# Expert loop: tokens copied and split ahead; last query block in halves; a home of their own for the row indices

## The chip, the cores and the metric

The kernel runs on one core of one Trainium2 chip, as one launch. The metric is the device time of one execution in microseconds (us). The core has TensorE (matmuls), VectorE, ScalarE, GpSimd and SyncE. Each has its own instruction stream; semaphores tie them together.

## The reference, cut to what matters

The layer works on x of 8 x 512 tokens with 256 channels, all in float32. It normalises the tokens and adds to x a windowed attention (16 heads of 16 channels, windows of 128 at a stride of 64, of which the output keeps the first four windows of each batch) and a mixture of experts (8 experts, the best two for each token):

```python
xn = _layernorm(x)
# attention: per window softmax(q k^T / 4) v, then @ w_out + b_out; o[:, :512]
scores = xn @ gate_w.T;  top 2 of 8, softmax over the two -> total_probs
h12 = xn @ w12[e].T;  h1, h2 = halves of 512
hidden = silu(h1) * h2
expert_out = hidden @ w3[e].T
x = x + attention(xn) + sum_e total_probs[e] * expert_out
```

The kernel computes only the chosen experts: tokens are sorted by expert into 71 tiles of 128 rows.

## The kernel before, in words

There are three stages. First come the layer norm, the transposes, the gates and attention of batches 0 and 1, during which the slots of the tokens and the list of row indices (the map) are made. Then the expert loop runs over 71 tiles. Then follow attention batches 2 to 7, in which the rows that the experts wrote to HBM (`ys_scratch`) are read back, scaled and added. Each batch has 8 units `u` (half a window's heads each), so that two units are one window of 128 queries.

The order is written out by hand, for each engine on its own.

Expert loop. A tile `j` is worked with buffers of parity `k`. GpSimd gathers 128 rows by `GIDX` into `XS` and scatters results by `SIDX`. TensorE, for each `k`: `up(j+1, 0)` (6 matmuls of 512 columns), `turn_hidden(j)` (4 transposes, line 1450), `up(j+1, 1)` (6 matmuls), `tokens(j+2)` (2 transposes, line 1428), `down(j)` (8 records). ScalarE: `high_part(j+2, half 0)` (line 829, the weights rounded to fp32r), `take_tanh(j+1)` (841), `take_ht(j)` (845), `high_part(j+2, half 1)`, `take_xt(j+2)` (849, copies the turned tokens to `XTS`), `take_y(j)` (855, into `SIDE` or `OTS`). VectorE: `low_part(j+2, half 0)` (350, weights minus their high part), the two products of `hidden(j+1)` (1172, then `tt` at 897), `low_xt(j+2)` (897, the tokens' low part, which releases `up(j+2, 0)`), `low_part(j+2, half 1)`. `high_part` and `low_part` first load the tile's expert number from `EJ` into a register (`weights_of`, lines 341 to 344). `up(j, half)` waits for `low_ready[half]`, and `up(j, 0)` also for `xt_free`.

Indices. `GIDX` and `SIDX` lie in `WORK`, where attention's `REST` is written by `split`. So `finish_map`, which writes them, stands a unit after `take_map` and waits for the parts of batch 2; and in batch 2 VectorE waits for `y_stored`, GpSimd's signal that all scatters have finished, before its first `split`.

End of a window. ScalarE copies the sums to `SIDE` and the counts to `DENS` (760, 761; in the trace `DENS` is part of `XN`). VectorE inverts `DENS` (1062), GpSimd multiplies into `OTS` (574), TensorE projects with `WOUT`, VectorE adds the total (`project`, 897 on `XN`). SyncE stores a batch of 512 rows with one transfer (`send`, 459). In the last batch VectorE projects window 2 before it inverts for window 3.

Of the kernel before, what the change touches and what calls it, by code (L numbers as in the profile page):

```python
# [97 lines left out]
def layer(nc, x, wqkv, bqk, bv, wout, bout, gate, wexp, out):  # L98
    with ExitStack() as ctx:
# [35 lines left out]
        WOUT = sb("WOUT", [P, NC_D, D])  # L135
        BOUT = sb("BOUT", [P, D])
        IDF = sb("IDF", [P, P])
        IDB = IDF[:].bitcast(BF16).rearrange("p (n k) -> p n k", k=2)[:, :, 1]
        SIDE = sb("SIDE", [P, D])
        OTS = sb("OTS", [P, NC_D, P])  # L140
# [24 lines left out]
        XS = work(2 * D).rearrange("p (b n) -> p b n", b=2)  # L165
        HTS = work(FH).rearrange("p (c n) -> p c n", c=FC)

        GIDX = work(XS_TILES).bitcast(U32)
        SIDX = work(XS_TILES).bitcast(U32)
        assert at <= NPART * nq + SPAN  # L170
        at = NPART * nq + 3 * SPAN + 2 * BANK
        HID = work(2 * FH).rearrange("p (b n) -> p b n", b=2)
# [182 lines left out]
        def _(sp):  # L355
# [142 lines left out]
                        send_later(b - 1 - FIRST_LATER, LATER[b - 1])  # L498
            send(LAST - 1)
            send_later(LAST - 1 - FIRST_LATER, LATER[LAST - 1])  # L500
            send(LAST)
            sp.wait_ge(out_done, 16 * B)


        @block.gpsimd
        def _(pool):
# [151 lines left out]
            for b in range(EXTRA, B):  # L658
                for n in range(NWIN):
                    if b in LATER:  # L660
                        later(b, n)
                    if b >= OWN:
                        own(b, n)
                    divide(b * NWIN + n)


        @block.scalar
        def _(act):
# [146 lines left out]
            for stage in range(2):  # L815
                if stage == 0:
                    for b in range(EXTRA):
                        batch(b)
                    take_shift(EXTRA % 2, 1)
                else:  # L820
                    for b in range(EXTRA, B):
                        batch(b)
                    break
                def high_part(j, k, half, used=None):

                    weights = weights_of(act, j, half)
                    if used is not None:
                        act.wait_ge((h1_full, h2_full)[half], used)
                    act.activation(WS[:, 1 - k, half, 0], weights, ACT.Copy  # L829
                                   ).then_inc(high_ready[half], 1)  # L830

                act.wait_ge(temps_done, 1)
                act.wait_ge(weights_in, 16 * E * CHUNKS)
                act.wait_ge(map_done, 1)
                high_part(0, 0, 0)
                high_part(0, 0, 1)
                act.wait_ge(probs_ready, c["ST"].now() + 2)

                def take_tanh(j, k):
                    act.wait_ge(h1_full, j + 1)  # L840
                    act.activation(HID[:, k, :], bank(2 * k), ACT.Tanh, scale=0.5).then_inc(tanh_ready, 1)

                def take_ht(j):
                    act.wait_ge(ht_full, j + 1)
                    act.activation(HTS, bank(6).rearrange("p (c n) -> p c n", c=FC), ACT.Copy).then_inc(ht_free, 1)  # L845

                def take_xt(j, k):
                    act.wait_ge(xt_full, j + 1)
                    act.activation(XTS[:, k, 0], bank(4 + k)[:, 0:D].rearrange("p (c n) -> p c n", c=NC_D),
                                   ACT.Copy).then_inc(xt_high, 1)  # L850

                def take_y(j, k, stored):
                    act.wait_ge(y_full, j + 1)
                    wait_some(act, y_out[k], 16 * stored)
                    act.activation(YS[k], bank(7)[:, 0:D], ACT.Copy).then_inc(ys_ready, 1)  # L855

                take_xt(0, 0)
                take_xt(1, 1)
                act.wait_ge(rows_out, 16 * EXTRA)
                high_part(1, 1, 0)  # L860
                take_tanh(0, 0)
                high_part(1, 1, 1)
                def tile(j, k, i):
                    high_part(j + 2, k, 0, j + 1)
                    take_tanh(j + 1, 1 - k)
                    take_ht(j)
                    high_part(j + 2, k, 1, j + 1)
                    take_xt(j + 2, k)
                    take_y(j, k, i)

                tile(0, 0, 0)
                tile(1, 1, 0)
                with act.Fori(1, SLOT_TILES // 2) as i:
                    for k in range(2):
                        tile(2 * i + k, k, i)
                last = SLOT_TILES - 1
                take_ht(last)
                take_y(last, last % 2, last // 2)
                act.wait_ge(ht_free, SLOT_TILES + 1)
                act.wait_ge(ys_ready, SLOT_TILES + 1)  # L880
                act.wait_ge(high_ready[1], XS_TILES)
                act.sem_inc(phase_done, 1)
                act.wait_ge(phase_done, 3)
# [3 lines left out]
        def _(dve):  # L887
# [170 lines left out]
            def invert():  # L1058
# [2 lines left out]
                dve.wait_ge(sides_ready, 2 * n)  # L1061
                dve.reciprocal(out=DENS, in_=DENS).then_inc(recip_ready, 1)  # L1062

            def project(b, n):
                t = b * TB + n
                total = BOUT[:] if b < OWN else XR[:, t, :]
                if b >= OWN:
                    dve.wait_ge(own_ready, (b - OWN) * TB + n + 1)
                dve.wait_ge(r_full, c["R"].add())
                tt(XN[:, t, :], R_BANK[:, 0:D], total, ALU.add).then_inc(r_free, 1)  # L1070
# [27 lines left out]
                link(tt(MA, MA, MAP[:, 1, :], ALU.add))  # L1098

            def finish_map():  # L1100
                dve.wait_ge(parts_ready, c["QK"].now())
                link(dve.tensor_copy(GIDX, MB))
                link(dve.tensor_copy(SIDX, MA))
                dve.sem_inc(map_done, 1)
# [4 lines left out]
            def batch(b, first=None):  # L1109
                last = b == LAST  # L1110
                pending = b and not ends(b - 1)
                for u in range(UNITS):
                    if b == EXTRA and u == 0:
                        dve.wait_ge(y_stored, 1)
                    if not last and u < 4:
                        split(u)
                    if not (last and u >= UNITS - 3):
                        take_max()
                    if u in (2, 4, 6) or (u == 0 and pending):
                        invert()  # L1120
                    if first == 0:
                        if u == 0:
                            route(1)
                        if u == 2:
                            take_ranks()
                            bases()
                        if u == 3:
                            experts_of_tiles()
                            shares()
                        if u == 4:  # L1130
                            dve.wait_ge(tiles_ready, 2)
                        if u >= 4:
                            tags(u - 4)
                        if u == UNITS - 1:
                            tags(4)
                    if first == 1:
                        if u < 2:
                            tags(5 + u)
                        if u == 0:
                            places()  # L1140
                        if u == 1:
                            tags(7)
                        if u == MAP_UNIT:
                            take_map()
                        if u == MAP_UNIT + 1:
                            finish_map()
                    if b == 0 and u == 3:
                        dve.wait_ge(xn_out, 64)
                    if u == 1 and pending:
                        project(b - 1, NWIN - 1)  # L1150
                    if u % 2 == 1 and u > 1:
                        project(b, u // 2 - 1)
                if not last:
                    c["W"].add(NWIN)
                if ends(b):
                    invert()
                    project(b, NWIN - 1)

            for stage in range(2):
# [7 lines left out]
                low_part(dve, 0, 0, 0)  # L1167
                dve.wait_ge(r_free, c["R"].now() + 1)

                def hidden(j, k):  # L1170
                    dve.wait_ge(tanh_ready, j + 1)
                    dve.scalar_tensor_tensor(out=HID[:, k, :], in0=HID[:, k, :], scalar=1.0, in1=bank(2 * k),  # L1172
                                             op0=ALU.add, op1=ALU.mult).then_inc(g_done, 1)
                    dve.wait_ge(g_done, j + 3)
                    dve.wait_ge(h2_full, j + 1)
                    tt(HID[:, k, :], HID[:, k, :], bank(2 * k + 1), ALU.mult).then_inc(hid_done, 1)
# [7 lines left out]
                low_xt(1, 1)  # L1184
                low_part(dve, 0, 0, 1)
                low_part(dve, 1, 1, 0)
                hidden(0, 0)
                low_part(dve, 1, 1, 1)
                with dve.Fori(0, SLOT_TILES // 2) as i:
                    for k in range(2):  # L1190
                        j = 2 * i + k
                        low_part(dve, j + 2, k, 0)
                        hidden(j + 1, 1 - k)
                        low_xt(j + 2, k)
                        low_part(dve, j + 2, k, 1)
                dve.wait_ge(low_ready[1], XS_TILES)
                dve.sem_inc(phase_done, 1)
# [4 lines left out]
        def _(pe):  # L1202
# [136 lines left out]
            def project():  # L1339
                pe.wait_ge(turned_ready, c["R"].now() + 1)  # L1340
                pe.wait_ge(r_free, c["R"].now() + 1)
                for ch in range(NC_D):
                    last = mm(R_BANK[:, 0:D], OTS[:, ch, :], WOUT[:, ch, :], ch == 0, ch == NC_D - 1)
                last.then_inc(r_full, 1)
                c["R"].add()
# [181 lines left out]
```

## Time and profile before

| | us |
|---|---|
| median of 3 runs (lowest, highest) | 746.48 (746.29, 747.36) |
| the profiled execution | 744.41 |
| its span, first to last instruction | 742.7 |
| TensorE busy in the span | 664.1 (89%) |
| VectorE | 572.3 (77%) |
| ScalarE | 505.2 (68%) |
| GpSimd | 297.9 (40%) |

Times below count from the span's start. The expert loop lies between about 158 and 541 us. PE is TensorE, PEld its weight loads, DVE VectorE, ACT ScalarE, POOL GpSimd, SP SyncE; a "q" behind a name is that engine's sequencer. The granted clock of TensorE was full through the loop and all but the last of the batches after it. Busy shares are averages over stages with different limits, so each edit is read in its own stage.

### The profile page before, as it was taken

The numbers are of one execution on the slowest core, as the hardware profiler recorded it, in microseconds if no ns is written. First come the engines' busy times: TensorE is split into PE (matmuls) and PEld (weight loads), VectorE is DVE, ScalarE is ACT, GpSimd is POOL, SyncE is SP. The second block draws the span as 40 slices with busy tenths as digits, with TensorE's granted clock in tenths as the row PEclk, the third lists the DMA queues.
The fourth block names the chain that finished last, engine by engine and source line by source line (L and its number), as shares of the span: only waits on it lengthen the run. The fifth ranks groups of instructions, "written<-read, shape, count | busy, mean of one in ns | idle before, by whom it ended". The sixth has DMA issues, their size and how long they took to land.

```text
span 742.7 us, 17175 instructions
## 1 busy us (share of the span) xinstructions
PE 664.1 (89%) x5648; PEld 515.0 (69%) x5649; DVE 572.3 (77%) x907; ACT 505.2 (68%) x880; POOL 297.9 (40%) x329
## 2 busy tenths in 40 slices
PE   0877776969999999999999999999989898999984
PEld 0655564848888878787878787788767676766663
DVE  4869899867777877777777777777857879797883
ACT  4545496566766666676767676767657787888884
POOL 3000470114445444444444454445311335666653
PEclk9999898999999999999999999999999999999998
DMA  8894677641111111111111111111147696875830
GB/s 290 277 261 139 168 269 251 195 173 41 46 54 45 50 47 57 42 49 49 57 42 50 49 54 45 49 49 49 42 135 206 183 263 187 278 197 174 223 118 29
DMA packets 66303, 92.56 MB, mean 125 GB/s; under 512 B 6384, under 2 KB 53360, under 8 KB 66256
## 3 DMA queue, kind: packets, MB, share of 16 engines
q1 hardware_dynamic: 57824, 70.40, 31.8%
q0 software_dynamic: 6864, 18.75, 8.0%
q10 hardware_dynamic: 1568, 2.76, 1.1%
q8 instruction: 31, 0.51, 0.3%
q14 instruction: 16, 0.13, 0.1%
HBM read 59.06 MB, written 32.83 MB: 124 GB/s over the span
## 4 chain that ended last, share of the span: by engine, by line
PE 64%; DVE 14%; ACT 9%; issue 7%; DMA 3%; POOL 2%; ACTq 0%; POOLq 0%; DVEq 0%; SPq 0%
PE PS L1206 57%; PE PS L1450 4%; DVE SMALL L903 4%; ACT WORK L753 3%; DVE XN L1062 2%; PE PS L1428 2%; DVE WALL L897 2%; ACT QS L748 1%; DMA XN<-in_x 1%; DVE WORK L972 1%; DVE WORK L965 1%; DMA KS<-parts_scratch 1%; DVE WALL L921 1%; ACT WORK L691 1%; ACT SIDE L760 1%
## 5 line engine op out<-in xcount | busy, mean ns | idle before, releaser
L350 DVE TENSOR_TENSOR WS<-WALL,WS 128x1024 fp32r<-128x1024 f32 x144 | 176.4, 1226 | 89.2 <-ACT WS L829 88.1
L1206 PE MATMUL PS<-WS,XTS 128*128 128x512 f32 x852 | 234.2, 410 | 2.7 <-DVE XTS L897 1.5
L1206 PEld LDWEIGHTS PS<-WS,XTS 128*128 128x128 f32 x852 | 149.6, 189 | 47.1 <-DVE XTS L897 14.2
L829 ACT ACTIVATE WS<-WALL 128x1024 fp32r x144 | 152.2, 1058 | 39.2 <-issue 36.7
L1206 PE MATMUL PS<-WALL,WORK 128*128 x568 | 136.0, 382 | 0.8 <-ACT WORK L845 0.8
L1206 PEld LDWEIGHTS PS<-WALL,WORK 128*128 128x128 f32 x568 | 102.3, 190 | 12.6 <-issue 1.0
L633 POOL DMA_INDIRECT WORK<-xn_scratch,WORK x72 | 100.8, 1400 | 24.7 <-issue 21.6
L574 POOL TENSOR_TENSOR OTS<-SIDE,XN 128x256 f32<-128x256 f32 x32 | 24.2, 755 | 210.8 <-DVE XN L1062 138.8
L637 POOL DMA_INDIRECT ys_scratch<-SIDE,WORK x36 | 41.9, 1165 | 117.1 <-ACT SIDE L855 117.1
L903 DVE TENSOR_REDUCE SMALL<-PS 128x8 f32<-128x1024 f32 x64 | 77.5, 1210 | 13.2 <-PE PS L1206 13.0
L753 ACT ACTIVATE WORK<-PS 128x512 f32<-128x512 f32 x128 | 69.4, 595 | 22.0 <-PE PS L1206 18.9
L748 ACT ACTIVATE QS<-PS 16x1024 bf16<-16x1024 bf16 x64 | 65.0, 1016 | 5.0 <-PE PS L1302 3.4
L637 POOL DMA_INDIRECT ys_scratch<-OTS,WORK x35 | 34.6, 988 | 71.1 <-ACT OTS L855 71.1
L1062 DVE RECIPROCAL XN<-XN 128x256 f32<-128x256 f32 x32 | 55.9, 1745 | 0.0
L1206 PEld LDWEIGHTS PS<-KS,QS 96*128 96x128 bf16 x512 | 32.9, 101 | 32.3 <-DVE SMALL L903 24.6
L1206 PE MATMUL PS<-KS,QS 96*128 96x128 bf16 x512 | 41.1, 226 | 12.8 <-DVE SMALL L903 12.0
L897 DVE TENSOR_TENSOR WORK<-WORK,PS 128x512 f32<-128x512 f32 x71 | 48.8, 687 | 2.5
L1206 PE MATMUL PS<-WOUT,OTS 128*128 128x256 f32 x128 | 37.3, 415 | 13.0 <-POOL OTS L574 12.3
L1172 DVE SCALAR_TENSOR_TENSOR WORK<-WORK,PS 128x512 f32<-128x512 f32 x71 | 48.3, 680 | 0.0
L1206 PE MATMUL PS<-WORK,VW 128*32 128x128 f32 x1024 | 42.7, 286 | 6.0 <-ACT WORK L753 6.0
L855 ACT ACTIVATE OTS<-PS 128x256 f32<-128x256 f32 x35 | 13.4, 384 | 46.7 <-PE PS L1206 46.7
L1206 PE MATMUL PS<-QS,KS 112*128 112x128 bf16 x512 | 40.4, 223 | 4.0 <-ACT QS L748 4.0
(137 smaller groups left out, 999.4 us busy)
## 6 DMA issues: line engine op xcount, KB each, us to landing
WALL<-in_wexp SPq DMA_DIRECT2D x28, 384.0 KB, 7.3
WALL<-ys_scratch SPq DMA_DIRECT2D x16, 512.0 KB, 7.1
parts_scratch<-WORK SPq DMA_DIRECT2D x32, 240.0 KB, 2.4
QS<-parts_scratch SPq DMA_DIRECT2D x16, 480.0 KB, 4.7
XN<-in_x SPq DMA_DIRECT2D x4, 1024.0 KB, 12.1
xn_scratch<-XN SPq DMA_DIRECT2D x4, 1024.0 KB, 7.5
WALL<-in_x SPq DMA_DIRECT2D x8, 512.0 KB, 5.9
KS<-parts_scratch SPq DMA_DIRECT2D x16, 240.0 KB, 3.9
```

The costliest lines, as they stand in the source:

```text
L350: eng.tensor_tensor(out=WS[:, 1 - k, half, 1], in0=weights, in1=WS[:, 1 - k, half, 0].bitcast(F32), op=ALU.subtract).then_inc(low_ready[ha ...
L633: pool.indirect_dma_start(XS[:, j % 2, :], None, xn_dram, bass.IndirectOffsetOnAxis(GIDX[:, j:j + 1], 0)).then_inc(xs_in[j % 2], 16)
L637: pool.indirect_dma_start(ys_dram, bass.IndirectOffsetOnAxis(SIDX[:, j:j + 1], 0), YS[j % 2], None).then_inc(y_out[j % 2], 16)
L748: act.activation(to, SHIFT_ROW.unsqueeze(1).to_broadcast([2 * HH, HH, WIN]), ACT.Copy).then_inc(t_free, 1)
L753: act.activation(PT[:, 2 * (u % 2) + q, :], ST_BANK[q], ACT.Exp, scale=SCALE).then_inc(probs_ready, 1)
L829: act.activation(WS[:, 1 - k, half, 0], weights, ACT.Copy).then_inc(high_ready[half], 1)
L897: return dve.tensor_tensor(out=o, in0=a, in1=b, op=op)
L903: return dve.tensor_reduce(out=o, in_=a, axis=AX_X, op=op, **kw)
L1062: dve.reciprocal(out=DENS, in_=DENS).then_inc(recip_ready, 1)
L1172: dve.scalar_tensor_tensor(out=HID[:, k, :], in0=HID[:, k, :], scalar=1.0, in1=bank(2 * k), op0=ALU.add, op1=ALU.mult).then_inc(g_done, 1)
L1206: return pe.matmul(o, a, b, start=start, stop=stop)
L1450: last = pe.transpose(bank(6)[:, f * P:(f + 1) * P], HID[:, k, f * P:(f + 1) * P], IDF[:])
```

## The change

In the expert loop ScalarE's `take_xt(j+2)` moves ahead of the second `high_part`, and VectorE's `low_xt(j+2)` moves between the two products of `hidden(j+1)`, which becomes `gated` and `hidden`. `GIDX` and `SIDX` become buffers of their own; `finish_map` runs in the same unit as `take_map`, without its wait, and VectorE's wait for `y_stored` is gone. For the last window VectorE inverts first, in two halves, GpSimd multiplies and TensorE projects by halves, and the last batch is stored in four transfers of 128 rows.

```diff
+        GIDX, SIDX = sb("GIDX", [P, XS_TILES], U32)[:], sb("SIDX", [P, XS_TILES], U32)[:]
-        GIDX = work(XS_TILES).bitcast(U32)
-        SIDX = work(XS_TILES).bitcast(U32)
@@ sync
-            send(LAST)
-            sp.wait_ge(out_done, 16 * B)
+            for n in range(NWIN):
+                sp.wait_ge(r_free, LAST * NWIN + n + 2)
+                t = LAST * TB + n
+                sp.dma_start(ov[:, t, :], XN[:, t, :]).then_inc(out_done, 16)
+            sp.wait_ge(out_done, 16 * (B - 1 + NWIN))
@@ gpsimd
-                    divide(b * NWIN + n)
+                    if b * NWIN + n < B * NWIN - 1:
+                        divide(b * NWIN + n)
+            pool.wait_ge(sides_ready, 2 * B * NWIN)
+            pool.wait_ge(r_full, B * NWIN - 1)
+            for k in range(NC_D):
+                pool.wait_ge(recip_ready, B * NWIN + k)
+                pool.tensor_tensor(out=OTS[:, k, :], in0=SIDE[:, k * P:(k + 1) * P], in1=DENS[:, k * P:(k + 1) * P],
+                                   op=ALU.mult).then_inc(turned_ready, 1)
@@ scalar, tile
                     take_ht(j)
+                    take_xt(j + 2, k)
                     high_part(j + 2, k, 1, j + 1)
-                    take_xt(j + 2, k)
@@ vector
+            def invert_last():
+
+                n = c["O"].add()
+                dve.wait_ge(sides_ready, 2 * n)
+                for k in range(NC_D):
+                    of = DENS[:, k * P:(k + 1) * P]
+                    dve.reciprocal(out=of, in_=of).then_inc(recip_ready, 1)
             def finish_map():
-                dve.wait_ge(parts_ready, c["QK"].now())
-                    if b == EXTRA and u == 0:
-                        dve.wait_ge(y_stored, 1)
                         if u == MAP_UNIT:
                             take_map()
-                        if u == MAP_UNIT + 1:
                             finish_map()
+                    if last and u == UNITS - 1:
+                        invert_last()
                     if u % 2 == 1 and u > 1:
                         project(b, u // 2 - 1)
                 if ends(b):
-                    invert()
+                    if not last:
+                        invert()
                     project(b, NWIN - 1)
@@ vector, expert loop (gated is the first product of the former hidden)
                         low_part(dve, j + 2, k, 0)
+                        gated(j + 1, 1 - k)
+                        low_xt(j + 2, k)
                         hidden(j + 1, 1 - k)
-                        low_xt(j + 2, k)
                         low_part(dve, j + 2, k, 1)
@@ tensor, project
                 for ch in range(NC_D):
+                    if c["R"].now() == B * NWIN - 1 and ch:
+                        pe.wait_ge(turned_ready, B * NWIN + ch)
```

## Rows read from the trace of the kernel before

**Rows 1.** The waits, 200 to 520 us: us in total, times, longest.
```profile
PEld PS L1206 <- DVE XTS L897: 10.9, 30, 0.4
```

**Rows 2.** The chain that ended last, 200 to 520 us: start, us, what.
```profile
210.49 3.42 PE PS L1206 x14
...
466.52 3.41 PE PS L1206 x14
```

**Rows 3.** The timeline of two tiles, 300 to 322 us: start, us, engine, instruction, idle before.
```profile
304.11 1.06 ACT L829 ACTIVATE WS<-WALL 128x1024 fp32r x1 [0.66 <-issue]
...
305.88 0.38 PEld L1428 LDWEIGHTS PS<-IDF,WORK 128*128 128x128 f32 x2
...
306.12 0.38 PE L1428 MATMUL PS<-IDF,WORK 128*128 128x128 f32 x2
306.29 1.59 PEld L1206 LDWEIGHTS PS<-WALL,WORK 128*128 128x128 f32 x8
...
306.97 0.39 ACT L849 ACTIVATE XTS<-PS 128x256 fp32r<-128x256 f32 x1
...
307.78 0.42 DVE L897 TENSOR_TENSOR XTS<-PS,XTS 128x256 fp32r<-128x256 f32 x1
...
308.25 1.23 PEld L1206 LDWEIGHTS PS<-WS,XTS 128*128 128x128 f32 x6 [0.36 <-DVE XTS L897]
...
308.41 0.39 ACT L855 ACTIVATE SIDE<-PS 128x256 f32<-128x256 f32 x1 [1.05 <-PE PS L1206]
...
309.15 1.06 ACT L829 ACTIVATE WS<-WALL 128x1024 fp32r x1 [0.35 <-issue]
...
310.35 1.23 DVE L350 TENSOR_TENSOR WS<-WALL,WS 128x1024 fp32r<-128x1024 f32 x1 [0.96 <-ACT WS L829]
...
311.36 0.38 PEld L1428 LDWEIGHTS PS<-IDF,WORK 128*128 128x128 f32 x2
...
311.70 1.60 PEld L1206 LDWEIGHTS PS<-WALL,WORK 128*128 128x128 f32 x8
...
313.45 1.23 PEld L1206 LDWEIGHTS PS<-WS,XTS 128*128 128x128 f32 x6
```

**Rows 4.** Line 343, the register loads: ns min/median/max.
```profile
L343 ACTq TENSOR_LOAD <-EJ x144: 273/279/493, 155.0 to 534.4; - x144
```

**Rows 5.** The timeline of batch 1, 128 to 170 us.
```profile
138.15 0.45 PEld L1206 LDWEIGHTS PS<-KS,QS 96*128 96x128 bf16 x8 [0.65 <-DVE SMALL L903]
...
138.42 0.19 DVE L1102 CAST WORK<-WALL 128x72 uint32<-128x72 f32 x1
```

**Rows 6.** The timeline of the loop's end and batch 2, 534 to 562 us.
```profile
542.91 0.53 ACT L691 ACTIVATE WORK<-PS,SMALL 128x320 bf16<-128x320 f32 x1 [1.55 <-PE PS L1206]
...
544.56 0.55 DVE L965 SCALAR_TENSOR_TENSOR WORK<-PS,SMALL,WORK 128x320 f32<-128x320 f32 x1 [6.12 <-POOLq L657]
```

**Rows 7.** The timeline of the kernel's end, 716 to 743 us.
```profile
733.82 0.38 ACT L761 ACTIVATE XN<-PS 128x256 f32<-128x256 f32 x1
...
734.64 0.42 DVE L897 TENSOR_TENSOR XN<-PS,WALL 128x256 f32<-128x256 f32 x1 [3.71 <-PE PS L1206]
...
734.98 1.74 DVE L1062 RECIPROCAL XN<-XN 128x256 f32<-128x256 f32 x1
736.86 0.72 POOL L574 TENSOR_TENSOR OTS<-SIDE,XN 128x256 f32<-128x256 f32 x1 [1.33 <-issue]
737.63 0.73 PEld L1206 LDWEIGHTS PS<-WOUT,OTS 128*128 128x128 f32 x4 [3.50 <-POOL OTS L574]
...
739.33 0.37 SPq L459 DMA_DIRECT2D out<-XN  x1
```

**Rows 8.** Sizes: line 1037; then DMA issues, with median us to landing.
```profile
L1037 DVE RECIPROCAL WALL<-WALL x1: 353/353/353, 89.6 to 89.6; 128x32 f32<-128x32 f32 x1
...
out<-XN SPq DMA_DIRECT2D x2, 512.0 KB, 3.0
...
parts_scratch<-WORK SPq DMA_DIRECT2D x32, 240.0 KB, 2.4
```

More of the change, by code:

```diff
@@ L1168, in _, with gated @@
                 dve.wait_ge(r_free, c["R"].now() + 1)
-                def hidden(j, k):
+                def gated(j, k):
                     dve.wait_ge(tanh_ready, j + 1)
@@ L1173, in hidden @@
                                              op0=ALU.add, op1=ALU.mult).then_inc(g_done, 1)
+                def hidden(j, k):
                     dve.wait_ge(g_done, j + 3)
@@ L1186, in _ @@
                 low_part(dve, 1, 1, 0)
+                gated(0, 0)
                 hidden(0, 0)
```

## The prediction

> **What bounds the kernel now.** I read the page's busy shares first, then the waits of the middle 320 us, then the chain of waits there, and last the instructions of one pair of tiles. TensorE is busy nearly throughout the expert loop, yet every second tile it stands still for 0.36 us until VectorE has written XTS [rows 1]. The chain that ended last is TensorE alone in that stretch; its pieces recur evenly: 24 pairs of tiles between 210.49 and 466.52, so 10.668 us for a pair, 5.334 for a tile [rows 2]. So a faster loop has to come out of TensorE's waits, and what VectorE and ScalarE do there matters by when it is ready. In [rows 3] the reader is to see the reason: the transposes of the token tile begin at 305.88 and end at 306.50, but ScalarE copies them only at 306.97, because it first splits off the high part of the next weights, and VectorE subtracts at 307.78, after the second product of HID. The result is there at 308.20, and TensorE's next group starts at 308.25. The stretch from the start of the down projection to that group is 308.25 - 306.29 = 1.96 us, and in the other tile, where nobody is named as late, 313.45 - 311.70 = 1.75 us. Of the 0.36 us of idle time only 0.21 are therefore to be had.
>
> **Part 1, the order in the expert loop.** Nothing is added; two operations of ScalarE and two of VectorE change places. ScalarE now copies the tokens at 306.50 + 0.05 = 306.55 (0.05 is what TensorE took to follow VectorE's 308.20), so until 306.94. VectorE subtracts about 0.14 later (the gap between ScalarE's end at 309.15 + 1.06 = 310.21 and VectorE's 310.35 [rows 3]): 307.08 to 307.50, before TensorE wants it at 308.04. The stall of 0.21 goes. A smaller one, 0.07, stays: the down projection starts 0.41 us after the transposes in one tile and 0.34 in the other [rows 3]; I read it as ScalarE's copy of HT, which hangs on the previous tile and isn't moved.
>
> What is late next? The high part of the second half of the weights stands behind the token copy now, and with it VectorE's low part and TensorE's next group but one. This is a closed chain from one tile's transposes to the next tile's, each link from [rows 3]: transposes to their end 0.62; signal 0.05; from the start of a short ScalarE copy that had to wait to the start of the high part behind it 0.74 (308.41 to 309.15); high part 1.06; signal 0.14; low part 1.23; signal 0.05; the group of six matmuls and step to the transposes 1.23 + 0.05. The sum is 5.17 us for a tile. TensorE without the stall needs (10.67 - 0.21) / 2 = 5.23. The chain stays below by 0.06 us: TensorE still bounds, but hardly. The 0.74 contains ScalarE's load of the tile's expert number into a register, 0.28 us [rows 4], and its address arithmetic. It used to hide behind the tanh and HT copies; now it stands in the open, because the copy before it waits.
>
> By these rows a pair becomes 10.67 - 0.21 = 10.46 us. Some 34.5 of the 35.5 pairs run in this steady state: 34.5 x 0.21 = 7.2 us. As two nearly equal chains never mesh perfectly, I take 7.0. Bounds: from 12.4 us gained (34.5 x 0.36, all the idle time) to a loss, which the rivals price.
>
> The Trainium skill (DMA: Bandwidth & Descriptors, section Latency and other measured facts) gives a register load from memory ("tensor_load") a floor of about 600 ns. By it, as an estimate, the closed chain would be 0.32 us longer, 5.49 a tile, and the change would lose about 11 us in the loop. The rows of the loads themselves say 273 to 493 ns with a median of 279 [rows 4], and speak against it here.
>
> **Part 2, the home of the indices, in batch 1.** The two casts of the map move one unit ahead, to just before a split. The first took 0.19 us [rows 5], the second is of the same size, and each is waited for: some 0.45. The split and the maximum behind it come so much later, and TensorE at 138.15 was waiting for just that maximum (0.65) [rows 5]. Nothing in the chain from there to the loop gives it back: TensorE's pieces follow one another up to the last projections. Cost 0.45, bounds 0 and 0.6. What an earlier map could bring starts no earlier: GpSimd's first gather also waits for batch 2's parts, and SyncE's expert loads stand behind the same batch's reads. The removed wait for the parts costs nothing now.
>
> **Part 3, VectorE's entry into batch 2.** VectorE waited 6.12 us for GpSimd's signal and began at 544.56. Without it the next to hold it is ScalarE's first part, 542.91 + 0.53 = 543.44 [rows 6], so a start at 543.50: 1.06 us earlier. TensorE's next long wait is for VectorE's first maximum and moves along. The second split is held by ScalarE's next part, which TensorE and not VectorE releases, and gains little; behind it the shift wavers between almost nothing and 1.06. VectorE's reciprocal of this batch follows its own chain and takes the full shift to the next parts. I take 1.0, bounds 0 and 1.1. ScalarE, GpSimd and SyncE keep their own waits for the scatters; the signal came just before 544.56, units ahead of ScalarE's first SIDE copy of the batch, so these hold nothing up.
>
> **Part 4, the last block in halves.** Before: ScalarE's DENS is ready at 733.82 + 0.38 = 734.20; VectorE first projects window 2 (0.42 from 734.64) and inverts from 734.98; TensorE starts at 737.63; SyncE issues the last 512 KB at 739.33, and the span ends at 742.7 [rows 7]. After: the inversion comes first. A reciprocal of 32 elements took 0.353 us and one of 256 1.745 [rows 7, 8], 6.2 ns an element, so one of 128 about 0.95. The halves run from 734.25 to 735.20 and (0.09 overlap) 735.11 to 736.06; the projection of window 2 runs behind them, from 735.98 to 736.40. TensorE waits for it, for the same bank, and starts at 736.45. GpSimd has halves to multiply: bounds 0.36 (half of a whole one's 0.72) and 0.72; at 0.45 the second is done at 736.2 + 0.45 = 736.65, before TensorE's second half at about 736.8 (half of its 0.73 on). So 1.18 earlier; 0.9 if GpSimd's halves cost as a whole one.
> Then the store: only 128 KB are left to go. 512 KB landed 3.0 us after issue (median in the last 27 us), 240 KB to memory 2.4 over the whole run [rows 8]. 128 KB lie at 2.0 to 2.4, and I take 2.25: gain 0.75, bounds 0 and 1.0. The three earlier stores (0.37 us each on SyncE) go out while the last window is computed. Total 1.9, bounds 0.9 and 2.2.
> The Trainium skill (DMA: Bandwidth & Descriptors, Anatomy of one DMA) fits a DMA as 2.0 us and its bytes at 436 GB/s; by it, as an estimate, 512 KB and 128 KB differ by 0.9 us, part 4 would be 2.1 and the total 0.15 lower. The landing rows agree in kind.
>
> **Sum.** -7.0 + 0.45 - 1.0 - 1.9 = -9.45 us. The profiled execution took 744.41 us (span 742.7) and would take 734.96; the median of the three runs before is 746.48, 2.07 above the profiled one, and I take the difference to it: 746.48 - 9.45 = 737.0 us.
>
> **Rivals.**
> A. The full stall goes, the HT wait too: 12.4 us in the loop, total -14.9, 731.6 us. For it: all 0.36 us are booked to XTS [rows 1]. Against: a boundary without a named wait shows 1.75 us as well.
> B. The wait only changes its name. The closed chain comes out at 5.33 a tile instead of 5.17, through signals slower by 0.03 to 0.05 at each of four hops. The loop stays at 10.67, and parts 2 to 4 alone count: -2.45, 744.0 us. For it: the distance of 0.06 us between the two chains. Against: each link is a measured row.
> C. The register load decides, and the kernel gets slower. If the gap behind the copy is the long one, 0.66 [0.66 <- issue at 304.11] and not 0.35 [rows 3], because the sequencer has more to do there, the chain is 5.17 + 0.31 = 5.48 and a pair 10.96: the loop loses 34.5 x 0.29 = 10 us, the total is +7.6, 754.1 us. The point of decision is 5.37 a tile (10.74 a pair), where the loop's loss eats the 2.45 us of the other parts. Against: the long gap belongs to the tile that carries the loop's branch, and the high part in question stands between no branch and its copy.
> C'. The same place with the load at 0.6 us: 5.17 + 0.32 = 5.49, 754.5 us; the page named in part 1 would have it. The load rows exclude it nearly.
> D. The new order finds no time at all because transposes come later than I think (a gather that lands late): then as B.
>
> **How the numbers follow.** Forecast 0.62 (734 to 740.5; its width is parts 2 to 4 and a loop between 5 and 9 us), A 0.10, B and D 0.18, C 0.08, C' 0.02. The range 732.5 to 744 leaves out C, C' and the far ends of A and B, some 0.17. Apart from no change can be told what lies beyond 0.2%, 1.5 us. Faster: forecast, A and nearly all of B and D, 0.87; same 0.04; slower 0.09.
>
> **What would show it.** In the loop: the pair at 10.46 us; ScalarE's token copy 0.05 us behind the transposes, the second high part 0.74 behind its start; no wait of TensorE for XTS; at most some 0.1 us for WS. Were TensorE to wait for WS in every tile, by more than 0.1 us, B or C holds. In batch 1: the maximum of unit 3 0.45 us later against its unit, and TensorE's wait there longer. At the loop's end: the first split of batch 2 0.06 us behind ScalarE's part, and no wait for GpSimd. At the end: reciprocals of 128 elements at 0.95 us, TensorE's last projection 1.2 us earlier against ScalarE's DENS copy, 128 KB landed in 2.25 us. The prediction is wrong if the pair is above 10.6 or below 10.4, or if batches 2 to 7 change by more than their start.

## The result and the profile after

The changed kernel takes 735.40 us (median of 4 runs, 734.33 to 735.70), the kernel before 746.88 beside it (4 runs). The ratio is 0.9844 with a 95% interval of 0.9827 to 0.9861: 11.5 us faster. The forecast was 737.0. Timed again in a later comparison, the ratio was 0.985 [0.9831, 0.987].

The profiled executions lie closer together: 744.41 us against 735.36, spans 742.7 and 733.6, so 9.1 us. The one of before was 2.5 us quicker than its median, the one of after sat on its median. The accounting below is of these two spans. "The pair" is, here and below, the time of two tiles of the expert loop, since the loop repeats itself every second tile.

The waits of the changed kernel between 200 and 520 us, all that the view lists for TensorE, VectorE and ScalarE (us in total, times, longest):

```profile
DVE WS L349 <- ACT WS L838: 73.2, 123, 0.9
...
ACT WS L838 <- issue: 47.9, 123, 0.7
ACT XTS L858 <- PE PS L1450: 30.8, 62, 0.6
...
ACT SIDE L864 <- PE PS L1226: 5.1, 31, 0.2
```

TensorE is in no row as a waiting engine: the 0.36 us of [rows 1] are gone. ScalarE now waits for TensorE's transposes before it copies the tokens (30.8 us, 62 times), which it did not have to do in this stretch before. The chain of waits in the same stretch:

```profile
201.32 3.20 PE PS L1226 x14
...
462.42 3.21 PE PS L1226 x14
```

Between these two pieces lie 25 pairs: 10.444 us a pair, where [rows 2] gave 10.668. One tile of the changed kernel, from its timeline:

```profile
300.02 0.37 PEld L1450 LDWEIGHTS PS<-IDF,WORK 128*128 128x128 f32 x2
...
300.36 1.59 PEld L1226 LDWEIGHTS PS<-WALL,WORK 128*128 128x128 f32 x8
...
300.67 0.38 ACT L858 ACTIVATE XTS<-PS 128x256 fp32r<-128x256 f32 x1 [0.61 <-PE PS L1450]
301.08 0.42 DVE L906 TENSOR_TENSOR XTS<-PS,XTS 128x256 fp32r<-128x256 f32 x1
301.32 1.06 ACT L838 ACTIVATE WS<-WALL 128x1024 fp32r x1 [0.27 <-issue]
301.43 0.68 DVE L906 TENSOR_TENSOR WORK<-WORK,PS 128x512 f32<-128x512 f32 x1
301.98 1.34 PEld L1226 LDWEIGHTS PS<-WS,XTS 128*128 128x128 f32 x6
...
302.53 1.23 DVE L349 TENSOR_TENSOR WS<-WALL,WS 128x1024 fp32r<-128x1024 f32 x1 [0.43 <-ACT WS L838]
...
303.92 1.23 PEld L1226 LDWEIGHTS PS<-WS,XTS 128*128 128x128 f32 x6
...
305.20 0.38 PEld L1450 LDWEIGHTS PS<-IDF,WORK 128*128 128x128 f32 x2
...
305.62 1.59 PEld L1226 LDWEIGHTS PS<-WALL,WORK 128*128 128x128 f32 x8
```

They answer to [rows 3]. The tokens' low part is ready at 301.50, while TensorE is still loading the down projection's weights until 301.95. Behind it the closed chain can be read off link by link: transposes at 300.02, copy 0.65 later, second high part 0.65 later, low part 1.21 later and 1.23 long, so ready at 303.76; TensorE takes it up at 303.92. That leaves 0.16 us.

The last 6 us, against [rows 7]:

```profile
727.22 0.38 ACT L770 ACTIVATE XN<-PS 128x256 f32<-128x256 f32 x1
...
727.63 1.76 DVE L1079 RECIPROCAL XN<-XN 128x128 f32<-128x128 f32 x2 [3.30 <-ACT XN L770]
...
728.89 1.03 POOL L672 TENSOR_TENSOR OTS<-SIDE,XN 128x128 f32<-128x128 f32 x2
729.31 0.36 DVE L906 TENSOR_TENSOR XN<-PS,WALL 128x256 f32<-128x256 f32 x1
729.79 0.73 PEld L1226 LDWEIGHTS PS<-WOUT,OTS 128*128 128x128 f32 x4 [2.26 <-POOL OTS L672]
...
731.03 0.42 DVE L906 TENSOR_TENSOR XN<-PS,WALL 128x256 f32<-128x256 f32 x1 [1.36 <-PE PS L1226]
```

Where the 9.1 us went, by the same events in both spans:

| stretch | before | after | change |
|---|---|---|---|
| start to VectorE's copy of the map | 132.93 | 132.97 | +0.04 |
| to TensorE's group behind the next maximum | 5.22 | 5.93 | +0.71 |
| to TensorE's first group of the expert loop | 21.66 | 21.75 | +0.09 |
| to its first projection of batch 2 | 381.63 | 375.19 | -6.44 |
| to ScalarE's last copy of the counts | 192.38 | 191.38 | -1.00 |
| to the end of the span | 8.9 | 6.4 | -2.5 |

The row for batches 2 to 7 is the one to "ScalarE's last copy of the counts".

The loop gives 34.5 x 0.224 = 7.7 us in its steady part and 6.44 in all, because its first tiles went slower here. The stretch from 155 to 166 us by windows, first before, then after (busy us of PE, PEld, DVE, ACT, POOL; granted clock, DMA share, GB/s):

```profile
155.00:166.00 11.00, 8.47 (x30) 5.43 (x30) 7.03 (x9) 6.81 (x10) 2.01 (x3) 0.84 0.25 80
```

```profile
155.00:166.00 11.00, 8.54 (x21) 6.18 (x22) 5.37 (x7) 6.14 (x8) 2.65 (x3) 0.53 0.30 94
```

TensorE's granted clock was 0.53 there and not 0.84. At 1.2 GHz it is 0.5, so some 10 of the 11 us went by at that level (2 x 0.47 x 11 = 10.3), and 3.5 in the kernel before (2 x 0.16 x 11). So the clock was full through the loop only behind its entry. Before this stretch TensorE had waited 3.4 us ahead of the last projection of batch 1 in both kernels. In the second profile of the changed kernel (`after_again`) the granted clock from 155 to 176 us was 0.92, as in the profile of before, where the first profile has 0.76; there the loop's stretch was 374.14 us, 7.49 less than before, and the whole span 732.0 us, 10.7 less.

### The profile page after: what moved, and what is told of

Its sections match the earlier page's. It is cut to its first block, busy times and chain, and to the rows that moved or that the text cites. A ratio compares the mean times of both kernels' runs of the same rounds, so it can differ in the third digit from the quotient of the medians.

```text
span 733.6 us, 17179 instructions
## 1 busy us (share of the span) xinstructions
PE 659.0 (90%) x5648; PEld 522.4 (71%) x5649; DVE 571.9 (78%) x908; ACT 520.9 (71%) x880; POOL 346.3 (47%) x330
## 4 chain that ended last, share of the span: by engine, by line
PE 65%; DVE 14%; ACT 9%; issue 7%; DMA 2%; POOL 2%; DVEq 0%; ACTq 0%; SPq 0%; POOLq 0%
PE PS L1226 58%; PE PS L1472 4%; DVE SMALL L912 4%; ACT WORK L762 3%; DVE XN L1071 2%; PE PS L1450 2%; DVE WALL L906 2%; ACT QS L757 2%; DMA XN<-in_x 1%; DVE WORK L981 1%; DVE WORK L974 1%; DMA KS<-parts_scratch 1%; ACT WORK L700 1%; DVE WALL L930 1%; ACT SIDE L769 1%
## 5 line engine op out<-in xcount | busy, mean ns | idle before, releaser
L1226 PE MATMUL PS<-WS,XTS 128*128 128x512 f32 x852 | 243.0, 421 | 1.9 <-DVE XTS L906 1.5
L1226 PEld LDWEIGHTS PS<-WS,XTS 128*128 128x128 f32 x852 | 157.1, 191 | 32.3 <-DVE XTS L906 1.9
L635 POOL DMA_INDIRECT WORK<-xn_scratch,GIDX x72 | 120.2, 1669 | 24.7 <-issue 21.6
L639 POOL DMA_INDIRECT ys_scratch<-OTS,SIDX x35 | 54.7, 1562 | 63.4 <-ACT OTS L864 63.4
L639 POOL DMA_INDIRECT ys_scratch<-SIDE,SIDX x36 | 50.6, 1407 | 70.2 <-ACT SIDE L864 70.2
L1071 DVE RECIPROCAL XN<-XN 128x256 f32<-128x256 f32 x31 | 54.1, 1745 | 0.0
L858 ACT ACTIVATE XTS<-PS 128x256 fp32r<-128x256 f32 x72 | 27.6, 383 | 36.9 <-PE PS L1450 36.9
```

Of the source, the lines that this page charges most:

```text
L635: pool.indirect_dma_start(XS[:, j % 2, :], None, xn_dram, bass.IndirectOffsetOnAxis(GIDX[:, j:j + 1], 0)).then_inc(xs_in[j % 2], 16)
L639: pool.indirect_dma_start(ys_dram, bass.IndirectOffsetOnAxis(SIDX[:, j:j + 1], 0), YS[j % 2], None).then_inc(y_out[j % 2], 16)
L1226: return pe.matmul(o, a, b, start=start, stop=stop)
```

## Experiments

All but the named edit is as in the kernel that each starts from. The pair is taken from recurring weight loads of TensorE between 200 and 510 us. "..." in a code cut stands for lines left out.

**1. The loop's order alone, and all but it.** The first is the kernel before with the loop's hunks of the diff, the second the changed kernel with them taken back.

```diff
 # e1_loop_order_alone: before, with ScalarE's
                     take_ht(j)
+                    take_xt(j + 2, k)
                     high_part(j + 2, k, 1, j + 1)
-                    take_xt(j + 2, k)
...
 # and VectorE's
                         low_part(dve, j + 2, k, 0)
+                        gated(j + 1, 1 - k)
+                        low_xt(j + 2, k)
                         hidden(j + 1, 1 - k)
-                        low_xt(j + 2, k)
```

> The kernel before with only the loop's new order (ScalarE's token copy ahead, VectorE's subtraction between the two products). Theory (the loop gives 7.5 us in the steady state, the other parts give their own): a pair of tiles takes 10.45 us, as in the changed kernel, and the kernel is 7 to 8 us faster than before, about 739.5. Rival (the parts help one another, and the loop alone brings less or the parts before it hide a part of it): less than 5 us.

> The changed kernel with the loop's old order. Theory: the pair stays at 10.67 us, the map's casts cost 0.8, VectorE's entry into batch 2 gives 1.0, the last block and its stores 2.5: 2.7 us faster than before, about 744. Rival (most of the gain came from the end and from disturbed runs of before): 5 us or more faster.

The loop alone: 738.33 us against 745.23, ratio 0.9897 [0.9872, 0.9923], 6.9 us faster by the medians and 7.7 by the ratio, pair 10.445. All but the loop: 741.21 against 745.23, ratio 0.9939 [0.9923, 0.9956], 4.0 us faster by the medians and 4.5 by the ratio, pair 10.669. The first agrees with the theory. The second does not: the interval reaches from 3.3 to 5.7 us, which leaves out the theory's 2.7 and holds the rival's 5. The three parts themselves measure what they should in its profile: 0.71 us more up to the group behind the maximum, 0.9 less over batches 2 to 7, 2.5 less at the end, 2.7 in all. So what is above that lies in stretches that this edit doesn't touch or in the executions of before beside it; which, stays open. The product of the ratios, 0.9837, is the whole change within its interval: that the parts help or hinder one another is not seen.

**2. Which of the two moves does it.**

```diff
 # e3_scalar_order_alone: before, ScalarE only
                     take_ht(j)
+                    take_xt(j + 2, k)
                     high_part(j + 2, k, 1, j + 1)
-                    take_xt(j + 2, k)
 # e4_vector_order_alone: before, VectorE only
+                        gated(j + 1, 1 - k)
+                        low_xt(j + 2, k)
                         hidden(j + 1, 1 - k)
-                        low_xt(j + 2, k)
```

> The kernel before with only ScalarE's token copy ahead of the second high part; VectorE keeps its order. Theory (TensorE waited for VectorE's second product, which stands ahead of the subtraction, not for ScalarE's copy): XTS is written no earlier, 0.36 us of idle time before the group stay, and the pair stays at 10.67 us. Rival (the token copy was what was late): the pair falls to 10.45.

> The kernel before with only VectorE's subtraction between the two products; ScalarE keeps its order. Theory: ScalarE's copy ends at 0.86 us behind the transposes' end, VectorE subtracts 0.14 later and is done 0.28 us earlier than before, which is more than the 0.21 us that TensorE lost: the pair falls to about 10.46 us without ScalarE's move. Rival (both moves are needed): the pair stays above 10.55 us.

ScalarE's move alone: pair 10.668, 746.66 us in one run against a median of 745.23 for before. Its waits between 200 and 500 us:

```profile
ACT XTS L849 <- PE PS L1428: 23.8, 43, 0.8
...
PEld PS L1206 <- DVE XTS L897: 10.2, 28, 0.4
```

ScalarE is early, and TensorE waits as before. VectorE's move alone: pair 10.446, 737.24 us, and among its waits

```profile
DVE XTS L897 <- ACT XTS L849: 13.6, 58, 0.3
```

VectorE now waits for ScalarE's copy, some 0.2 us each time, and TensorE waits for nobody. So the 7.7 us are VectorE's; the copy ahead adds nothing to them and only puts the register load into the open. Both pairs are from one profile each; the same pair came out within 0.01 us in every profile of kernels with the same loop.

**3. The closed chain: its cost taken away and doubled.**

```diff
 # e6_one_register_load_a_tile: the changed kernel; expert() is the load alone,
 # and a high_part that is given `at` loads nothing
                 def tile(j, k, i):
-                    high_part(j + 2, k, 0, j + 1)
+                    at = expert(j + 2)
+                    high_part(j + 2, k, 0, j + 1, at)
...
                     take_xt(j + 2, k)
-                    high_part(j + 2, k, 1, j + 1)
+                    high_part(j + 2, k, 1, j + 1, at)
 # e7_register_load_doubled: the changed kernel
                     take_xt(j + 2, k)
+                    act.value_load(EJ[0:1, bass.ds(j + 2, 1)], min_val=0, max_val=E - 1)
                     high_part(j + 2, k, 1, j + 1)
```

> The changed kernel in which ScalarE loads a tile's expert number once and uses it for both halves, so that the second high part follows the token copy at 0.3 instead of 0.65 us. Theory (TensorE bounds the loop, the closed chain over the copy, the high part and the low part stays below it): the pair stays at 10.44 us. Rival (the closed chain bounds): it falls by up to 0.7 us a pair.

> The changed kernel with a second, unused register load between ScalarE's token copy and its second high part. One load with its address arithmetic takes about 0.5 us of the sequencer. Theory (closed chain, in the changed kernel 5.07 us a tile: copy 0.65 behind the transposes' start, high part 0.65 later, low part 1.21 later, 1.23 long, group and step 1.33): 5.57 to 5.62 us a tile, a pair at 11.15 to 11.25, TensorE waits for WS in each tile, and the whole kernel is slower than before, about 760. Rival (slack takes it up): the pair stays under 10.7 us.

One load a tile: pair 10.438 against 10.445, 733.45 us in one run. The load was not what bounds. The doubled load: pair 11.215, 760.93 us in one run, 13.5 slower than the run of before beside it. Its timeline:

```profile
301.66 1.23 PEld L1227 LDWEIGHTS PS<-WS,XTS 128*128 128x128 f32 x6 [0.41 <-DVE WS L349]
...
303.58 0.38 ACT L858 ACTIVATE XTS<-PS 128x256 fp32r<-128x256 f32 x1 [0.82 <-PE PS L1451]
...
304.76 1.06 ACT L838 ACTIVATE WS<-WALL 128x1024 fp32r x1 [0.81 <-issue]
...
305.98 2.58 DVE L349 TENSOR_TENSOR WS<-WALL,WS 128x1024 fp32r<-128x1024 f32 x2 [0.96 <-ACT WS L838]
```

The high part stands 1.18 us behind the start of the copy instead of 0.65, and TensorE waits for WS in every tile (54 times in 300 us). A load and its arithmetic cost 0.53 us. The chain then needs 5.61 us a tile (11.215 / 2), and 5.61 - 0.53 = 5.08 without it: the 5.07 that the links of the changed kernel add up to. The chain is real, and in the changed kernel it stays 0.14 us a tile below TensorE's 5.22.

**4. The map's casts a unit later.**

```diff
                         if u == MAP_UNIT:
                             take_map()
+                        if u == MAP_UNIT + 1:
                             finish_map()
```

> The changed kernel with the map's two casts back in the unit after the map, with no wait for the parts. Theory (the casts ahead of the split delayed the chain into the expert loop by 0.74 us): the maximum that TensorE waits for comes 0.7 us earlier against the copy of the map, and TensorE's first group of the loop 0.7 to 0.8 us earlier against the map's copy than in the changed kernel. Rival (the delay came from something else in batch 1 that the change moved): that distance stays as in the changed kernel.

From the map's copy to TensorE's group behind the maximum 5.24 us (5.93 in the changed kernel), to the first group of the loop 26.98 (27.68): 0.7 us back. The first of these distances is 5.92 to 5.94 us in all seven profiles with the casts ahead of the split and 5.22 to 5.24 in all seven with them behind it. The changed kernel's rows show the price: two casts and a wait of the engine for its own last one, in front of the split.

```profile
135.57 0.20 DVE L1118 CAST GIDX<-WALL 128x72 uint32<-128x72 f32 x1
...
135.80 0.20 DVE L1119 CAST SIDX<-WALL 128x72 uint32<-128x72 f32 x1
...
136.27 0.55 DVE L974 SCALAR_TENSOR_TENSOR WORK<-PS,SMALL,WORK 128x320 f32<-128x320 f32 x1 [0.27 <-DVE SIDX L1119]
...
138.90 0.45 PEld L1226 LDWEIGHTS PS<-KS,QS 96*128 96x128 bf16 x8 [1.29 <-DVE SMALL L912]
```

TensorE's wait was 0.65 us in [rows 5] and is 1.29.

**5. VectorE's wait in front of batch 2.**

```diff
                 for u in range(UNITS):
+                    if b == EXTRA and u == 0:
+                        dve.wait_ge(y_stored, 1)
```

> The changed kernel with VectorE's wait for the scatters' signal in front of batch 2. Theory (the removed wait gave 1.0 us, and batches 2 to 7 only moved): TensorE's first projection of batch 2 to ScalarE's last copy of the counts takes 192.4 us, as before the change, against 191.4 in the changed kernel. Rival (the shift is swallowed by ScalarE's parts): 191.4 to 191.6.

First projection of batch 2 to ScalarE's last copy of the counts: 192.40 us with the wait, 192.38 before, 191.38 in the changed kernel. The 1.0 us is this wait. Its size is not known to a tenth: this stretch took 191.98 to 192.44 us in the five profiles with the wait and 190.73 to 191.63 in the nine without it. Inside the stretch the gain is uneven at first: TensorE's second projection of batch 2 comes only 0.28 us earlier against the first than before, the fourth 0.80, and all from batch 3 on about 1.0. The changed kernel's rows:

```profile
537.30 0.53 ACT L700 ACTIVATE WORK<-PS,SMALL 128x320 bf16<-128x320 f32 x1 [1.55 <-PE PS L1226]
...
538.04 0.55 DVE L974 SCALAR_TENSOR_TENSOR WORK<-PS,SMALL,WORK 128x320 f32<-128x320 f32 x1 [4.54 <-ACT WORK L700]
```

VectorE follows ScalarE's part 0.21 us after its end, not the 0.06 that I had given it.

**6. The last batch in one store.**

```diff
-            for n in range(NWIN):
-                sp.wait_ge(r_free, LAST * NWIN + n + 2)
-                t = LAST * TB + n
-                sp.dma_start(ov[:, t, :], XN[:, t, :]).then_inc(out_done, 16)
-            sp.wait_ge(out_done, 16 * (B - 1 + NWIN))
+            send(LAST)
+            sp.wait_ge(out_done, 16 * B)
```

> The changed kernel whose last batch is stored in one transfer of 512 KB again; the halves stay. Theory (the store's size gave 1.2 us): from VectorE's last addition to the end of the span 3.8 us, as before, against 2.6 in the changed kernel. Rival (the halves alone moved the end): the same 2.6.

From VectorE's last addition to the end 3.8 us, as expected, against 2.6; the rows of the issue in this and in the changed kernel (median us to landing at their end):

```profile
out<-XN SPq DMA_DIRECT2D x2, 512.0 KB, 2.9
```

```profile
out<-XN SPq DMA_DIRECT2D x4, 128.0 KB, 1.7
```

The store's size is worth 1.2 us. The rest of the 2.5 lies ahead of VectorE's last addition: from the copy of the counts to it 5.05 us before, 3.81 in the changed kernel and in this one. Two edits share it, the inversion ahead of window 2's projection and the halves, and no run takes them apart. By the rows the inversion begins 0.41 us behind the start of the copy and not 1.16, so some 0.75 of the 1.24 may be the order's. The one time of the whole kernel can't tell the store's size apart (735.30 us).

**7. The register load ahead, and the casts later.** ScalarE loads a tile's number once, ahead of the copy of the expert's result, so that the first high part no longer waits for the load; the casts are a unit later, as in experiment 4. The second version differs in that the token copy stands in its old place.

```diff
 # e8_loads_ahead_map_later (the old tile and the casts left out)
+                def front(j, k, at):
+                    high_part(j + 2, k, 0, j + 1, at)
+                    take_tanh(j + 1, 1 - k)
+                    take_ht(j)
+                    take_xt(j + 2, k)
+                    high_part(j + 2, k, 1, j + 1, at)
                 def tile(j, k, i):
+                    at = expert(j + 3)
+                    take_y(j, k, i)
+                    front(j + 1, 1 - k, at)
 # e9_vector_order_loads_ahead: as e8, and in front()
-                    take_xt(j + 2, k)
                     high_part(j + 2, k, 1, j + 1, at)
+                    take_xt(j + 2, k)
```

> The changed kernel once more, timed beside the two versions below: 0.984 to 0.986 of before, pair 10.44 us. It also shows whether TensorE's half clock at the loop's start lasts 3.4 or 10.2 us in another execution.

> The changed kernel with ScalarE's register load once a tile and ahead of the copy of the expert's result (so that the first high part follows that copy at once), and the map's casts a unit later. Theory (what is left of TensorE's stalls is 0.08 us a pair, for ScalarE's copy of HT, which hangs on the load in front of the first high part): the pair falls to 10.36 us, 2.8 us over the loop, with 0.8 from the casts 3.6 us faster than the changed kernel. Rival (TensorE's own issue sets 10.44): the pair stays, and only the 0.8 us remain.

> As the version with the loads ahead, but with ScalarE's token copy behind the second high part, as before the change. Theory (VectorE's order alone took the stall away): the pair is the same as in that version, within 0.01 us, about 10.36. Rival (with the first high part earlier the copy's place matters): more than 10.40.

| | us (median) | ratio to before, 95% interval | pair |
|---|---|---|---|
| the changed kernel again | 733.84 | 0.9850 [0.9831, 0.9870] | 10.444 |
| loads ahead, map later | 731.76 | 0.9816 [0.9797, 0.9834] | 10.387 |
| the same, copy in its old place | 732.38 | 0.9828 [0.9806, 0.9850] | 10.369 |

The first version is 2.1 us below the changed kernel by the medians, where 3.6 were expected. Its five runs (730.30 to 732.15) all lie below the four of the changed kernel beside them (733.32 to 734.01), so a gain is likely, though the intervals of the two ratios just touch. The second is 1.5 us below by the medians, but its runs (730.18 to 733.84) and its interval overlap the changed kernel's, so its gain is not shown. The pair fell by 0.06 and 0.08, which is 2.0 and 2.6 us over 34.5 pairs, beside 0.7 for the casts in both: the wait for HT was there and is gone. The tile that showed it, in the version with the loads ahead:

```profile
305.75 0.39 ACT L870 ACTIVATE SIDE<-PS 128x256 f32<-128x256 f32 x1 [0.48 <-PE PS L1240]
306.03 1.05 ACT L844 ACTIVATE WS<-WALL 128x1024 fp32r x1
...
308.48 0.38 PEld L1464 LDWEIGHTS PS<-IDF,WORK 128*128 128x128 f32 x2
...
308.82 1.60 PEld L1240 LDWEIGHTS PS<-WALL,WORK 128*128 128x128 f32 x8
```

The high part follows the copy at 0.28 us instead of the 0.74 and 1.05 of before, and the down projection starts 0.34 behind the transposes, in this tile and in the one before it (0.35). The two orders of ScalarE can't be told apart by their times; by the pair, of one profile each, the old place is better by 0.02, against what I had written (within 0.01).

## Why the prediction was right

**Part 1.** Forecast: a pair at 10.46 us, 7.0 us in all. Measured: 10.444, 7.7 in the steady part; the 0.2 us that I had taken off because nearly equal chains would not mesh were not needed. That only 0.21 of the 0.36 us of idle time were to be had holds: TensorE's distance from down projection to next group is now 1.62 us, and its six loads take 1.34 instead of 1.23, which together are the 2.96 of the undisturbed tile (1.75 + 1.23 = 2.98 in [rows 3]). The wait for HT stayed at 0.08, as said. The closed chain was put at 5.17 us and measures 5.07; the link that was too dear is the one from the copy to the high part, 0.65 and not 0.74, and the wait that I had read it from carries one more address step, of 43 ns in the trace. Experiment 3 shows the chain and its price. What the prediction missed: it called ScalarE's move part of the cure. Its own numbers (ScalarE's copy ends at 307.36 in [rows 3], VectorE could be done by 307.92, TensorE comes at 308.04) would have told that VectorE's move is enough, and experiment 2 shows it. So the rivals B, C and C', which price the chain over the copy ahead of the high part, were a risk that the gain didn't need.

**The loop's entry** was taken as unchanged. Here it cost about 1.3 us (7.7 - 6.44), with TensorE at 1.2 GHz for some 10 us where the profile of before had 3.5. I don't take that for a part of the change: the version with ScalarE's move alone has the long stretch too, at the old pace of the loop (382.81 us from the first group to batch 2), and the changed kernel's second profile has a short one (374.14). Long against short, the stretch to batch 2 thus differs by 1.2 us at the old pace (382.81 and 381.63) and by 1.1 at the new (375.19 and 374.14); like against like, the new pace gives 7.5 and 7.6. The version with all but the loop's order has the full clock there but lost as much, 383.03 us, while ScalarE waited 3.9 us for the store of the rows.

**Part 2.** Forecast +0.45, measured +0.71, shown by experiment 4. The step that was mis-sized is "some 0.45 with the wait between": behind the second cast stands another wait of 0.27 us, ahead of the split.

**Part 3.** Forecast 1.0, measured 1.00 in one profile of the changed kernel and 0.79 in the other (191.59 us), shown by experiment 5. VectorE begins 0.15 us later behind ScalarE's part than said. The shift wavered within batch 2 as said (0.28 at the second projection) and was back at about 1.0 from batch 3 on (0.7 to 0.8 in the second profile).

**Part 4.** Forecast 1.9, measured 2.5. From the copy of the counts to TensorE's last projection 2.57 us against 3.81 of [rows 7]: 1.24, forecast 1.18. The reciprocals of 128 elements took 0.90 and 0.95 us, GpSimd's halves 0.45 each. The store gave 1.2 where 0.75 stood: 128 KB landed in 1.7 us, below the 2.0 to 2.4 that I took from larger transfers in a busier stretch. By the fit of the Trainium skill (DMA: Bandwidth & Descriptors, Anatomy of one DMA), 2.0 us and the bytes at 436 GB/s, it would as an estimate be 2.3 us; the page states that fit for transfers that GpSimd issues, and this one is SyncE's, so the measurement decides.

**The rivals.** A (all the idle time back) is out: the pair would be 10.31. B (the wait changes its name) and D (late transposes) are out: TensorE has no wait, and the pair is not 10.67. C and C' are out at 5.07 a tile (by its own terms C' is 754.7 us, not the 754.5 of the text), but the place was the right one: with the load doubled the kernel is slower than before. The floor of about 600 ns that the Trainium skill (DMA: Bandwidth & Descriptors, section Latency and other measured facts) gives a register load doesn't hold here: the loads took 279 ns (median), and one with all its arithmetic 0.53 us.

**The sum.** -9.45 forecast for the profiled execution, -9.1 measured: the loop's entry (1.3), the casts (0.26) and two stretches that I had taken as unchanged (0.13) took 1.7 us more, the steady loop and the end gave 1.3 more. That the two sums lie so close is in part luck. Against the changed kernel's second profile, whose entry is short as in the profile of before, the span fell by 10.7 us. The medians fell by 11.5, since the profiled execution of before was 2.5 us quicker than its median. The granted clock goes with that: of the 18 executions of the kernel before whose mean clock is on record, the three at 0.981 or 0.982, the profiled one among them, took 742.42 to 744.41 us, and the fifteen at 0.972 to 0.979 took 744.71 to 747.42. None of the fifteen was profiled, so in which stretch they lost the clock is not shown; a long entry would be one such stretch.

## What to carry to other kernels

When the bounding engine waits for the last of several operations of another one, ask first what stands directly ahead of that last operation. Moving that one thing was enough here, and the second move put a register load onto a closed chain. A closed chain from tile to tile is worth adding up link by link before a reorder: the distance between its length and the bounding engine's is what the next edit may cost. Idle time booked to a wait holds what the engine would have needed anyway: compare it with the same boundary where nobody is late. A difference of two profiles holds what differed in the clock too: compare two executions with the same granted clock in the stretch in question, or say that you can't.

## What the runs showed of the hardware

A register load of a tile's number, with its address arithmetic, costs ScalarE's sequencer 0.53 us (experiment 3). It was hidden where the operation ahead of it had not waited, and stood in the open after one that had: the high part started 0.65 us behind the start of such a copy, 1.18 with a second load between, and 0.28 with none (experiments 3 and 7).

A store of 128 KB to HBM, issued by SyncE at the kernel's end, landed in 1.7 us, one of 512 KB in 2.9 to 3.0 (experiment 6, [rows 8]).

TensorE's half clock at the loop's entry, behind a wait of 3.4 us, lasted some 3.5 us in the profile of before and 10.3 in that of after (granted clock of 155 to 176 us 0.92 and 0.76). In the other twelve profiles that clock was 0.76 to 0.79 in ten, 0.92 in one (`after_again`) and 1.00 in one (all but the loop's order). The long stretch cost 1.1 to 1.2 us against the short one, by one pair of profiles at each pace of the loop. What decides between them was not tried.
